# A Mamba-2 mixer with a LoRA feed-forward: group sums, additions, scores and the mask product take other places

## What is computed

```python
gate, hBC, dt = split(hidden @ in_proj_w.T)            # 8192 | 8192 + 2 * 1024 | 128
hBC  = silu(causal_conv4(hBC) + conv_b)                # hs (128 heads x 64), B and C (8 groups x 128)
dt   = softplus(dt + dt_bias);  X = hs * dt            # chunks of 128 tokens
M    = (C @ B.T) * exp(segsum(-exp(A_log) * dt))       # "scores" times decay, lower triangle
y    = M @ X + C @ prev_states * exp(A_cs) + D * hs
xg   = y * silu(gate)
xr   = xg * rsqrt(mean(xg * xg over 1024 channels) + eps)   # 8 groups of channels
out  = (xr * norm_weight) @ out_proj_w.T
out += x_norm @ W.T + b + top-1 LoRA(x_norm)
```

## Time and profile before

| | |
|---|---|
| median of 3 runs | 1745.4 us (1744.01 to 1745.47) |
| profiled execution | 1747.96 us, of which the span 1746.2 us |
| PE busy | 1668.7 us, 96% of the span |
| DVE, ACT, POOL busy | 78%, 68%, 63% |
| PE's granted clock, mean | 0.981 of full speed |
| chain that ended last | PE 75%, DVE 15%, ACT 4%, issue 4% |
| transfers | 212.03 MB, 16 DMA engines busy for 36.8% |

### The profile page before, as it was taken

The page is one execution under the profiler, slowest core; times in us unless marked ns, Lnnn a source line. Parts: engine busy times, 40 slices in busy tenths (PEclk is TensorE's granted clock), DMA queues, the critical chain, the costliest instruction groups (busy, mean ns, idle before and its releaser), DMA issues.

```text
span 1746.2 us, 28887 instructions
## 1 busy us (share of the span) xinstructions
PE 1668.7 (96%) x9694; PEld 1371.7 (79%) x9694; DVE 1354.4 (78%) x2388; ACT 1191.5 (68%) x2442; POOL 1095.1 (63%) x1384
## 2 busy tenths in 40 slices
PE   6889999999999999999898899999999999999997
PEld 5677878787888878788687688787878787888875
DVE  5777787878778787878878677878787878787785
ACT  2457777777777777777634577777767777777773
POOL 5235676667666766676663366676676667666764
PEclk9989999999999999999989899999999999999998
DMA  4133443344334434433222333443443344334431
GB/s 146 38 128 117 140 132 133 118 139 136 122 125 140 137 114 133 139 129 115 77 85 73 126 125 133 139 130 114 139 139 127 117 139 139 125 120 139 139 105 45
DMA packets 82146, 212.03 MB, mean 121 GB/s; under 512 B 11024, under 2 KB 27408, under 8 KB 81744
## 3 DMA queue, kind: packets, MB, share of 16 engines
q1 hardware_dynamic: 82000, 210.20, 36.8%
HBM read 207.01 MB, written 3.15 MB: 120 GB/s over the span
## 4 chain that ended last, share of the span: by engine, by line
PE 75%; DVE 15%; ACT 4%; issue 4%; DMA 0%; POOL 0%; SPq 0%; DVEq 0%; POOLq 0%; ACTq 0%
PE bh L505 20%; PE bg L505 18%; PE bo L662 15%; PE by L635 6%; DVE cv L691 5%; PE bt L627 4%; PE bt L649 4%; PE bt L671 2%; DVE acc L709 2%; ACT cv L282 2%; DVE mt L910 2%; PE bo L505 1%; DVE S L716 1%; DVE by L902 1%; PE bo L601 1%
## 5 line engine op out<-in xcount | busy, mean ns | idle before, releaser
L436 POOL TENSOR_TENSOR wl<-raw,wh 128x256 fp32r<-128x256 f32 x584 | 537.0, 950 | 131.8 <-ACT wh L278 131.8
L489 POOL TENSOR_TENSOR wol<-raw_o,woh 128x256 fp32r<-128x256 f32 x256 | 184.3, 741 | 487.0 <-ACT woh L403 487.0
L691 DVE SCALAR_TENSOR_TENSOR cv<-bh,par_sb,cv 128x511 f32<-128x511 f32 (+2 forms) x408 | 304.7, 747 | 197.1 <-ACT cv L282 192.0
L291 ACT ACTIVATE mt<-cs_row,cs_tok 128x128 f32<-128x128 f32 x1024 | 324.3, 389 | 0.0
L662 PE MATMUL bo<-woh,xh 128*128 128x512 f32 x512 | 212.5, 415 | 1.4 <-POOL xl L477 1.4
L662 PE MATMUL bo<-woh,xl 128*128 128x512 f32 x512 | 201.7, 394 | 0.0
L662 PE MATMUL bo<-wol,xh 128*128 128x512 f32 x512 | 199.9, 390 | 0.0
L364 ACT ACTIVATE xh<-xg 128x512 fp32r<-128x512 f32 x128 | 81.0, 633 | 162.8 <-DVE xg L906 162.8
L287 ACT ACTIVATE bh<-cv 128x512 f32<-128x512 f32 x136 | 81.8, 602 | 155.7 <-DVE cv L691 155.7
L477 POOL TENSOR_TENSOR xl<-xg,xh 128x256 fp32r<-128x256 f32 x256 | 181.7, 730 | 5.8 <-ACT xh L364 5.8
L894 DVE SCALAR_TENSOR_TENSOR sg<-tg,bg 128x512 f32<-128x512 f32 x128 | 87.9, 686 | 125.5 <-ACT tg L399 125.5
(11 more groups left out here) (159 smaller groups left out, 3351.0 us busy)
## 6 DMA issues: line engine op xcount, KB each, us to landing
raw<-in_w_step SPq DMA_DIRECT2D x128, 512.0 KB, 3.6
cs_row<-cs_rows SPq DMA_DIRECT2D x128, 512.0 KB, 4.4
raw_o<-in_w_out SPq DMA_DIRECT2D x128, 256.0 KB, 2.7
ec_row<-ec_rows SPq DMA_DIRECT2D x256, 96.0 KB, 3.7
raw<-in_w_bc SPq DMA_DIRECT2D x16, 512.0 KB, 3.7
acc<-in_x SPq DMA_DIRECT2D x2, 1024.0 KB, 5.7
mt<-in_w_ffn SPq DMA_DIRECT2D x2, 1024.0 KB, 6.7
out_dram<-acc SPq DMA_DIRECT2D x2, 1024.0 KB, 4.7
```

The lines of the kernel that those rows point to most:

```text
L291: e = act.activation(mt[:, m % 2, h, chunk(j)], cs_row[:, m % 2, h, chunk(j)], ACT.Relu, bias=cs_tok[:, b, j, 2 * m + h:2 * m + h + 1], sc ...
L436: e = pool.tensor_tensor(wl[:, n % 2, part], raw[:, n % 2, part], wh[:, n % 2, part].bitcast(F32), ALU.subtract)
L489: e = pool.tensor_tensor(wol[:, 1 - u, part], raw_o[:, 1 - u, part], woh[:, 1 - u, part].bitcast(F32), ALU.subtract)
L691: dve.scalar_tensor_tensor(out=cv[:, u, k:], in0=src[:, 0:L - k], scalar=par_sb[:, un % UNITS, TAPS - 1 - k:TAPS - k], in1=cv[:, u, k:], o ...
```

## The change

Four things change their place; no arithmetic is added or taken away.

1. The eight matmuls of the squares write four columns of bt that the state product leaves free (384 to 387), not of by. PE issues them ahead of the output projection, not behind the transposes, and waits there for POOL's sum of squares. The wait for xg goes; the next transposes into bt wait for ms. DVE reads ms ahead of yo in the same pass, POOL makes rr in the same pass.
2. The four additions of a finished group stand at the head of the next pass, behind the mask product and ahead of the first tap, not behind the skip term.
3. The scores of group g follow two groups late, behind the projections of group g + 2; those of groups 6 and 7 stand inside step 0, behind its two projections. The ninth pass goes. The mask of the scores and ACT's copy (`take_b`) move likewise, and silu of group g waits for the transposes of group g - 2.
4. The mask product of step m - 1 stands behind xd and xt at the head of pass m, not at the tail of pass m - 1.

```diff
@@ ACT
+            def take_b(b, g):
+                act.wait_ge(t_bt, did(b * GROUPS + g))
+                act.activation(btok[:, g], bo[3][:, 0:NS * P].rearrange("p (c k) -> p c k", c=NS),
+                               ACT.Copy).then_inc(a_bt, 1)
...
+                    if g >= 2:
+                        take_b(b, g - 2)
...
                         last_tap(un, u, bh)
+                        if m == 0:
+                            take_b(b, GROUPS - 2)
...
+                        if m == 0:
+                            take_b(b, GROUPS - 1)
@@ POOL
-                    if m - 2 >= PER_GROUP and (m - 2) % PER_GROUP == 0:
-                        rms((n - 2) // PER_GROUP - 1)
...
                         e.then_inc(p_wol, 1)
+                    if m >= PER_GROUP and m < STEPS and (m - 2) % PER_GROUP == PER_GROUP - 1:
+                        rms((n - 2) // PER_GROUP)
@@ PE
+            def scores(b, g):
+
+                n, u = b * GROUPS + g, g % 2
+                if g == 0:
+                    pe.wait_ge(pv, b * PRO_DVE + PRO_DVE)
+                pe.wait_ge(v_h2, did(b * UNITS + 2 * g + 1))
+                pe.wait_ge(v_g, did(n - 1))
+                for j in range(NJ):
+                    mm = pe.matmul(bo[2][:, chunk(j)], h2[:, u, chunk(j)], ct[:, g, chunk(j)], start=True, stop=True)
+                mm.then_inc(t_gm, 1)
+                pe.wait_ge(a_bt, did(n - 1))
+                for c in range(NS):
+                    mm = pe.transpose(bo[3][:, chunk(c)], h2[:, u, chunk(c)], ident[:, :])
+                mm.then_inc(t_bt, 1)
...
+                    if g >= 2:
+                        scores(b, g - 2)
...
                         project(bh, b, step(b, m) % 2, 0).then_inc(t_hs, 1)
+                        if m == 0:
+                            scores(b, GROUPS - 2)
...
                         project(bg, b, step(b, m) % 2, 1).then_inc(t_g, 1)
+                        if m == 0:
+                            scores(b, GROUPS - 1)
...
                         mm.then_inc(t_off, 1)
+                    if has(m - 2) and (m - 2) % PER_GROUP == PER_GROUP - 1:
+                        pe.wait_ge(p_sqa, squares(b, m - 2))
+                        for j in range(NJ):
+                            mm = pe.matmul(bt[:, NS * P + j:NS * P + j + 1], sqa[:, chunk(j)], ones[:, 0:1],
+                                           start=True, stop=True)
+                        mm.then_inc(t_ss, 1)
...
                         pe.wait_ge(v_off, did(n - 1))
+                        if m >= PER_GROUP and (m - 2) % PER_GROUP == PER_GROUP - 1:
+                            pe.wait_ge(v_ms, did((n - 2) // PER_GROUP))
...
-                    if has(m - 2) and (m - 2) % PER_GROUP == PER_GROUP - 1:
-                        pe.wait_ge(p_sqa, squares(b, m - 2))
-                        pe.wait_ge(v_xg, did(min(n - 1, b * STEPS + STEPS - 1)))
-                        for j in range(NJ):
-                            mm = pe.matmul(by[:, j:j + 1], sqa[:, chunk(j)], ones[:, 0:1], start=True, stop=True)
-                        mm.then_inc(t_ss, 1)
@@ DVE
+                    if g >= 2:
+                        dve.wait_ge(t_bt, did(b * GROUPS + g - 2))
+                    silu_conv(un, 0, bank_b[g % 2], h2[:, g % 2, :])
+                    silu_conv(un + 1, 1, bank_c[g % 2], ct[:, g, :])
+                    if g >= 2:
+                        mask_scores(b, g - 2)
...
-                    if ended is not None:
-                        mean_square(ended)
...
                                           ALU.mult).then_inc(v_x, 1)
+                        dve.wait_ge(a_ex, did(n - 1))
+                        dve.wait_ge(v_g, did(b * GROUPS + min(m - 1, GROUPS - 1)))
+                        dve.tensor_tensor(mt[:, 1 - u], mt[:, 1 - u],
+                                          gt[:, (m - 1) % GROUPS, :].unsqueeze(1).broadcast_to([P, 2, L]),
+                                          ALU.mult).then_inc(v_m, 1)
+                    if ended is not None:
+                        add_group(b, ended)
                     if has(m):
                         tap(un, u, bh, 1)
...
-                    if ended is not None:
-                        add_group(b, ended)
...
                         dve.wait_ge(t_t, did(n - 2))
+                        if m < 2:
+                            dve.wait_ge(t_bt, did(b * GROUPS + GROUPS - 2 + m))
+                        if m == 0:
+                            mask_scores(b, GROUPS - 2)
                         silu_conv(un, u, bh, h2[:, u, :])
...
                     if has(m - 1):
+                        if m >= PER_GROUP and (m - 2) % PER_GROUP == PER_GROUP - 1:
+                            mean_square((n - 2) // PER_GROUP)
                         dve.wait_ge(t_off, did(n - 1))
...
-                    if has(m):
-                        dve.wait_ge(a_ex, did(n))
-                        dve.wait_ge(v_g, did(b * GROUPS + min(m, GROUPS - 1)))
-                        dve.tensor_tensor(mt[:, u], mt[:, u],
-                                          gt[:, m % GROUPS, :].unsqueeze(1).broadcast_to([P, 2, L]),
-                                          ALU.mult).then_inc(v_m, 1)
+                    if m == 0:
+                        mask_scores(b, GROUPS - 1)
```

More of the change, by code:

```diff
@@ L630, in _ @@
                         pe.wait_ge(v_xg, did(n - 2))
-                        if m - 1 >= PER_GROUP and (m - 3) % PER_GROUP == PER_GROUP - 1:
-                            pe.wait_ge(v_ms, did((n - 3) // PER_GROUP))
                         for j in range(NJ):
@@ L824, in _ @@
                 decays_and_route(b)
-                for g in range(GROUPS + 1):
+                for g in range(GROUPS):
                     un = b * UNITS + 2 * g
-                    if g < GROUPS:
-                        for k in range(1, TAPS):
-                            tap(un, 0, bank_b[g % 2], k)
-                        for k in range(1, TAPS):
-                            tap(un + 1, 1, bank_c[g % 2], k)
+                    for k in range(1, TAPS):
+                        tap(un, 0, bank_b[g % 2], k)
+                    for k in range(1, TAPS):
+                        tap(un + 1, 1, bank_c[g % 2], k)
                     if g == 1:
```

88 lines of the change are left out of this document (31 added, 57 removed).

## The result

The changed kernel takes 1704.13 us (median of 4 runs, 1702.03 to 1705.19), the kernel before 1744.7 beside it (4 runs): ratio 0.9768, 95% interval 0.9751 to 0.9785, so 40.6 us less. The forecast was 1698.1 in a range of 1688 to 1711. The profiled execution of after took 1703.99, of which the span is 1702.2; that of before 1747.96, so the two traces are 44.0 apart. What follows compares traces, stretch by stretch.

What follows compares the result with a forecast made beforehand. PE, busy 1668.7 of 1746.2 us, was taken as the bound, so only its waits could shrink. Gains of 32.6 + 10.8 + 2.7 + 1.2 = 47.3 took the median from 1745.4 to 1698.1, range 1688 to 1711.

Steps and rivals of the forecast that it cites:

- Scores two groups late: Groups of B and C: PE's waits of 5.3 and 4.05 go; step 1 starts 14.3 us earlier a batch.
- the three waits for bo[2]: PE's new waits in each batch: 1.15 us at scores of group 1, 1.75 at group 6, 0.2 at group 7.
- Steps 1 and 2: Each batch: step 1 loses a half clock, 1.6 us; step 2 its wait for xt with restart, 0.4.
- Group ends: Three steps at each of 14 group ends: 35.95 us against 36.72, 0.77 less each, 10.8 together.
- the term of 1.38 for the mask product: Head of a step: mask product takes 1.38 us behind xd and xt, ending at T + 2.8, before L635 and first tap.
- Rival 5: Mask product, held up by POOL's weight split, comes too late for L635: 1717 or 1837 us; 3 in 100 for ending slower.
- The end of the first batch: xt earlier without the mask product in front, half clock gone, less waits for mask and POOL's last sum: net 2.7 us.
- The tail: Last steps gain 2.4 us; 1.2 set against it for a half clock behind PE's 2.7 idle: net 1.2.
- (1): Rival: PE's short waits halve the clock, some 1.6 us each: 1704.5 or 1727 us; 15 in 100.
- (2): Rival: ACT and DVE pace the groups of B and C more slowly than counted: 1707 to 1712 us; 12 in 100.
- (4): Rival: the scores' two groups of distance shrink to one, PE's waits return elsewhere, only steps gain: 1730 us; 3 in 100.
- (3): Rival: additions cost at the head what they cost now, as L649 waits for S: 1706 us; 8 in 100.

Runs made afterwards that it cites:

- the squares behind the transposes: Changed kernel with the group's squares summed behind the transposes again and the root behind POOL's split: 1698.79 us, 0.9746 of before.
- pieces of 128: Changed kernel with GpSimd's split of the step weights in pieces of 128 columns instead of 256: 1693.1 us, 0.9722 of before.
- pieces of 512: Changed kernel with GpSimd's split of the step weights in pieces of 512 columns instead of 256: 1713.33 us, 0.9831 of before.
- the mask product at the tail: Changed kernel with the mask product back at the tail of the pass, all else as changed: 1696.6 us, 0.9726 of before.
- The scores alone: Kernel before with only the scores moved two groups late: 1715.77 us, 0.9838 of before.
- the fastest one: Changed kernel with additions two and two, split in pieces of 128, last batch's last squares behind its output projection: 1679.69 us, 0.9628 of before.

## Why the prediction was right, and where it was off

**Scores two groups late: right, 26.3 of 28.6.** The chain that the prediction followed through DVE and ACT is the one that sets the pace; two of the three waits for bo[2] came where it put them, a little shorter. The second batch reached step 1 13.7 earlier (14.3 predicted), the first 12.6, where the half clock in its first groups lasted longer than before.

**Steps 1 and 2: 2.6 of 4.0.** The wait for yo of 2.14 stayed, as said. The prediction took from the earlier trace rows that no half clock follows it. It did not follow in the first batch and did in the second, after the same wait (windows of after, first batch, then second):

```profile
125.20:130.20 5.00, 4.96 (x38) 1.00 0.62 186
```

```profile
958.86:963.86 5.00, 5.00 (x18) 0.66 0.62 197
```

The step that failed is reading one row as a rule: 1.94 has 0.65 behind it in one kernel and 1.00 in another, 2.14 has both in one trace. Nine of the kernels here have this wait for yo, of 1.9 to 2.1, once in each batch, and in 10 of these 18 places a half clock follows.

**Group ends: the sum was right, 10.8, its parts were not.** The first step was as forecast (12.17 for 12.2) and the third too (11.30 for 11.35). The second is 12.71 and not 12.4. The step that failed is the term of 1.38 for the mask product, which takes 1.81 there: it ends at T + 3.17 instead of T + 2.8, the additions at T + 5.80 instead of 5.45, S at T + 8.66 instead of 8.4. The prediction had asked of the root ahead of the split only whether the split would be done in time; it didn't ask what the split, begun 1.0 later, would then lie over. So the three give 14 x 0.55 = 7.7. The other 3.1 come from "an ordinary step keeps its length": every second one had lasted 11.4, held by xt, and all are 11.30 now. The prediction held 11.3 to 11.4 in its hand and set no gain for it. That 7.7 and 3.1 make just the 10.8 of the forecast is luck.

**The mask product's 1.38 was itself a delay.** The prediction used that row to say that POOL gives way. The runs show that both give way. Without a piece of the split beside it the mask product takes 1.22 (the rows of the kernel with the squares behind the transposes, above). Where a piece is running when it begins, it ends 1.08 to 1.10 after the end of that piece: in 124 of the 128 mask products of before and of after, and in all 128 with pieces of 128 and with pieces of 512. In before it began at 816.82, inside the split's first piece (the first two pieces on POOL):

```profile
816.38 0.74 POOL L436 TENSOR_TENSOR wl<-raw,wh 128x256 fp32r<-128x256 f32 x1
```

```profile
817.08 1.72 POOL L436 TENSOR_TENSOR wl<-raw,wh 128x256 fp32r<-128x256 f32 x1
```

It had 0.30 to wait, and 0.30 + 1.08 are the 1.38. At its new place it begins just behind a piece's start, has 0.6 to 0.7 to wait and takes 1.7 to 1.8; the means are 1.31, 1.70 and 2.05 with the pieces' size. The second row is the other direction: the piece behind the one that was running takes 1.72 and not 0.7, since it waits for the mask product. So the 3.81 of the split are three pieces of 0.7 and one of 1.7, and not four of 0.95 as the prediction read them. Rival 5 had the right mechanism. Its price of 0.95 was too high, as the mask product lost 0.33 more than in before in the mean and 0.43 in the second step; its slack of 0.8 covered that in ordinary steps, and in pieces of 512 it began to show there. It costs in the second step, where there is no slack.

The page "SBUF — State Buffer" of the Trainium skill, section "Who interferes with whom", states that the two engines share a port pair under an exclusive lock, that VectorE contends with two inputs in SBUF and GpSimd when it reads SBUF, and that the one that starts first blocks the other for its whole instruction. For the long pieces the runs agree, both ways: the mask product waits for a piece of POOL, and POOL's root takes 2.04 instead of 1.03 where it comes behind a mask product's start. In one point they don't: the root that starts at 774.72, 0.12 ahead of the mask product, does not hold it up at all. With the mask product at the tail it starts 0.5 ahead at the groups' ends, and the mask product still takes 1.22. So the root doesn't keep the lock for its whole 1.03. The prediction had cited this page and then let the 1.38 speak against half of it.

**The end of the first batch: 5.4 instead of 2.7.** The mechanism was right (xt ahead of the mask product), and so nearly was its size: without the mask product at the tail, the three steps go from 15.96 to 13.28, from 12.33 to 11.50 and from 21.21 to 20.16, which is 4.6 where 3.7 had been set. The scores alone leave the first two near their old length (15.84, 12.30) and so does the mask product at the tail, so it is the mask product's place. PE's wait for POOL's last sum was 0.79, as counted (1.0). The remainder is a half clock ahead of the second batch's groups that no term priced. Up to the first of them it lasts 6.7 us in before and 2.6 in after (windows of before, then of after), which is 2.0 of the 5.4, and the kernels that share this code differ there as much among themselves:

```profile
885.90:892.60 6.70, 6.70 (x34) 0.50 0.00 0
```

```profile
864.60:867.20 2.60, 2.60 (x14) 0.50 0.00 0
```

**The tail: -1.2 instead of 1.2.** Two terms failed. The idle time of 2.65 ahead of the squares was foreseen (2.7), but 1.2 was set for a half clock that cost 1.6: the output projection behind it ran at 0.58, for the most part at 0.43 a matmul instead of 0.23, and took 4.4 instead of 2.9. And the 2.4 of the last steps were about 1.0. Without a half clock in the last step, the last step and the end take 33.9 with the scores alone and 32.9 with the squares behind the transposes; that is what the mask product's place gives. To hide ms and rr behind the output projection gave nothing, since PE idles 2.65 ahead of the squares for it and 1.38 otherwise. The last 0.4 is the half clock in the last step, which cost 1.2 in before (35.0 against 33.9) and 1.6 in after (36.2 against 34.6).

**The last 2.6.** The prediction kept the distance between the profiled run and the median of before. After has none: its profiled run is its median. Together: the trace gave 44.0 of 47.3, and the distance took 2.7 more, which makes 1704 for 1698. That the trace's sum is so near is in part luck: the end of the first batch gave 2.7 more than was forecast, the tail 2.4 less.

**Rivals.** (1) did not come: behind none of the four short waits for bo[2] and of the 14 of about 1.05 for S does a half clock stand; the one in the second batch stands behind the wait of 2.14. (2) and (4) did not come. (3) is what the additions did, and worse: at the head they cost 0.4 more per group's end than behind the skip product. Within the change that was hidden by what the squares and the mask product gave to the same three steps.

## What to carry to other kernels

When a row's duration is used to say that two engines don't disturb each other, look first for the same instruction with the other engine out of its way: the undisturbed 1.22 was what the 1.38 had to be read against. And an instruction that is moved on an engine off the critical path moves what stands behind it: the root ahead of the split cost the mask product 0.6. A part moved to the head of a step must be followed to the next thing that is late on the same engine. Taking half of it ahead and half behind the critical operand gave more than either place. And what a part is worth depends on what stands beside it: to put the squares back cost nothing in the steps of the changed kernel, and 21 us in the fastest one, where it also made the root late.

## What the runs showed that was not expected

- The mask product takes 1.22 us undisturbed, and ends 1.08 us after the end of the GpSimd piece that was running when it began: means of 1.31, 1.70, 2.05 for pieces of 128, 256, 512 columns. Cutting the same work on GpSimd finer made the kernel some 8 us faster (5.7 by the steps in question) without touching the critical engine.
- It works the other way too: GpSimd's 128x4 root took 2.04 us behind a started mask product, 1.03 elsewhere, and a piece of 0.7 us took 1.72.
- Whether a half clock follows a wait of TensorE of 1.9 to 2.1 us is not set by the wait alone. The same wait had a granted clock of 1.00 and of 0.66 behind it in one trace, and a half clock followed in 10 of 18 such places. What else decides was not found; no run here was made to tell it.
